# A new order of the work at two change-overs, and slot tables counted in tiles, in an attention / expert / mixing block

## The reference

```python
x = x + attn_a(layernorm(x), W_q, W_k, W_v, W_o)      # causal linear attention, H = 64
x = x + ffn(layernorm(x), router_W, router_b, W1, b1, W2, b2)
x = x + attn_b(layernorm(x), time_decay, mixes, Wk, Wv, Wr, Wo)   # scan over time, then a gate
x = x + ffn(layernorm(x), router_W, router_b, W1, b1, W2, b2)     # the same weights again

def attn_a(x):              # phi(u) = elu(u) + 1
    q, k, v = phi(x @ W_q), phi(x @ W_k), x @ W_v
    S_t = S_{t-1} + k_t v_t^T;  z_t = z_{t-1} + k_t
    return ((S_t q_t) / max(z_t . q_t, 1e-6)) @ W_o

def ffn(x):                 # 8 experts, each token to one of them
    probs = softmax(x @ router_W + router_b);  top1 = argmax(probs)
    h = relu(x @ W1[top1] + b1[top1])                  # 128 -> 512
    return probs[top1] * (h @ W2[top1] + b2[top1])     # 512 -> 128

def attn_b(x):
    state_t = x_t + state_{t-1} * d;  prev_t = state_{t-1}
    v_in, r_in = mixes of x_t and prev_t
    return sigmoid(r_in @ Wr^T) * ((v_in @ Wv^T) @ Wo^T)
```

## Time and profile before

| | before |
|---|---|
| median of 3 runs | 356.7 us |
| profiled execution, its time | 358.61 us |
| profiled execution, span from first to last instruction | 356.9 us |
| mean granted TensorE clock | 0.94 of full |
| PE busy | 301.4 us (84%) |
| DVE busy | 256.4 us (72%) |
| POOL busy | 202.2 us (57%) |
| ACT busy | 137.4 us (39%) |

### The profile page before, as it was taken

How to read it: one execution, slowest core, us unless ns; L and a number is a source line. 1 busy time by engine, 2 the same in 40 slices (tenths; PEclk the granted TensorE clock), 3 DMA queues, 4 the chain that set the end, 5 groups by cost and what they waited for, 6 DMA issues and landing times.

```text
span 356.9 us, 9023 instructions
## 1 busy us (share of the span) xinstructions
PE 301.4 (84%) x2137; PEld 255.4 (72%) x2137; DVE 256.4 (72%) x1046; ACT 137.4 (39%) x407; POOL 202.2 (57%) x247
## 2 busy tenths in 40 slices
PE   1898999975778899999996979678696999999970
PEld 1366676654668799999934768567395989999960
DVE  4748799999587877787626778686458787777750
ACT  3645565421223344444304653422122334454420
POOL 4834378885545774455425456887423676545550
PEclk9999999995898999999998999989859899999995
DMA  7992001105636788777144000111644778877500
GB/s 201 251 200 27 1 18 39 40 30 180 154 110 174 211 219 237 196 207 167 38 121 116 0 3 23 38 38 48 195 121 123 211 206 229 227 195 200 155 8 0
DMA packets 42610, 44.22 MB, mean 124 GB/s; under 512 B 7120, under 2 KB 29905, under 8 KB 42560
## 3 DMA queue, kind: packets, MB, share of 16 engines
q10 hardware_dynamic: 11808, 20.71, 22.6%
q1 hardware_dynamic: 26176, 14.39, 17.4%
q0 software_dynamic: 4576, 8.54, 6.7%
HBM read 33.06 MB, written 11.53 MB: 125 GB/s over the span
## 4 chain that ended last, share of the span: by engine, by line
PE 53%; DVE 18%; POOL 11%; issue 8%; DMA 3%; ACT 3%; DVEq 1%; SPq 0%; POOLq 0%; ACTq 0%
PE pair L1324 17%; PE pair L1310 14%; POOL sorted L449 5%; PE bank L1310 4%; DVE stats L706 3%; PE pair L1154 2%; POOL rstd L408 2%; PE pair L1178 2%; PE pair L1215 2%; PE pair L1136 2%; DVE hT L1022 2%; POOL rows L423 1%; PE pair L1144 1%; PE pair L1200 1%; PE pair L1301 1%
## 5 line engine op out<-in xcount | busy, mean ns | idle before, releaser
L1324 PE MATMUL pair<-w2s,hT 128*128 x624 | 86.3, 283 | 1.7 <-ACT hT L655 0.6
L449 POOL DMA_INDIRECT sorted<-rows,place x64 | 65.3, 1020 | 29.0 <-issue 14.7
L1324 PEld LDWEIGHTS pair<-w2s,hT 128*128 128x128 f32 x624 | 78.4, 197 | 4.0 <-issue 3.8
L1310 PE MATMUL pair<-xsT,w1s 128*128 128x128 f32 x472 | 69.4, 286 | 1.0 <-ACT xsT L649 0.8
L1310 PEld LDWEIGHTS pair<-xsT,w1s 128*128 128x128 f32 x472 | 62.6, 202 | 1.7 <-ACT xsT L649 1.7
L462 POOL DMA_INDIRECT out<-ys,xs x39 | 38.1, 976 | 32.3 <-DVE ys L1033 25.8
L462 POOL DMA_INDIRECT x_mid<-ys,xs x39 | 38.1, 978 | 31.7 <-DVE ys L1033 27.4
L1022 DVE TENSOR_SCALAR hT<-pair,w1s 128x128 f32<-128x128 f32 x156 | 47.0, 343 | 3.4 <-PE pair L1310 3.2
L1014 DVE SCALAR_TENSOR_TENSOR xs<-b2b,xs 128x128 f32<-128x128 f32 x78 | 27.6, 353 | 21.7 <-DVE xsn L1006 19.5
L1033 DVE SCALAR_TENSOR_TENSOR ys<-pair,xs 128x128 f32<-128x128 f32 x78 | 27.2, 349 | 13.7 <-PE pair L1324 13.5
L706 DVE BATCH_NORM_STATS2 stats<-rows 128x6 f32<-128x128 f32 x128 | 27.5, 277 | 10.4 <-DMA rows<-x_mid 6.7
(11 more groups left out here) (159 smaller groups left out, 513.6 us busy)
## 6 DMA issues: line engine op xcount, KB each, us to landing
w1s<-in_L_ffn_W_b ACTq DMA_DIRECT2D x78, 258.0 KB
xs<-sorted SPq DMA_DIRECT2D x78, 66.0 KB, 3.4
rows<-in_L_attn_a_x SPq DMA_DIRECT2D x8, 256.0 KB, 4.0
w2s<-in_L_ffn_W SPq DMA_DIRECT2D x8, 256.0 KB, 5.7
rows<-x_mid SPq DMA_DIRECT2D x8, 256.0 KB, 4.8
sorted<-pad SPq DMA_DIRECT2D x30, 66.0 KB, 3.5
sorted<-rows,place POOLq DMA_INDIRECT x64, 2.4
x_mid<-ys,xs POOLq DMA_INDIRECT x39, 3.5
```

The lines of the kernel that those rows point to most:

```text
L449: pool.indirect_dma_start(sorted_rows[l], bass.IndirectOffsetOnAxis(ap=place[:, t:t + 1], axis=0), rows[:, t, :], None).then_inc(s_sent[l] ...
L1310: mm = nc.tensor.matmul(bank[2 + 2 * half + i % 2][:, c * P:(c + 1) * P], w1s[i % NW][:, f:f + P], xsT[i % NB][:], start=True, stop=True)
L1324: mm = nc.tensor.matmul(bank[6 + i % 2][:, 0:P], hT[i % NB][:, c], w2s[:, bass.ds(e, 1), c, :].rearrange("p o d -> p (o d)"), start=(c == ...
```

## The change

It alters eight things; nothing of what is computed changes.

1. **Tables in tiles.** `slot_table` counts in tiles of 128 rows. Part 0 has 3 instructions (5 before), part 1 has 3 (3 in stage 0, 5 later), part 2 has 3. What a stage passes to the next (`cover`, `taken`, `gone`, `behind`) is a part 3 of its own with 3 instructions in stage 0 and 4 in stage 1. SP's load takes a tile number. At the start POOL makes one more small constant (`capt8`) and DVE two (`whole8`).
2. **First change-over, DVE.** Slot 8 becomes `last_attn_slot`: `denominators(6)`, `mask_scores(7)`, the first table (until then at the end of slot 7), `add_state(7)`, `placed(4)`, `add_attention(6)`, `choose(5)`.
3. **First change-over, into the experts.** `placed(5)` comes after the first three `norm_rows`, and `moments(6)` comes with `moments(7)` after `hidden(0)`.
4. **First change-over, PE.** `project_out(7)` is the last but one step of attention slot 8, ahead of `count(5)`. Before `first(0)` PE waits for `placed(5)` to have read the counts.
5. **ACT, both.** Only 2 of the first 4 weight loads come before the last copy (`evac_o(7)`, `evac_x2T(7)`), the other 2 after it.
6. **Second change-over, DVE.** The first table comes ahead of `choose(5)`, `moments(6)` goes into the experts, `keep_logits` comes ahead of `hidden(0)`.
7. **Second change-over, PE.** `logits(6)` comes ahead of `count(5)`; `keep_clock(6)` becomes `keep_clock(2)`; `transpose_x2(7)` comes ahead of the two `turn`s and `logits(7)` ahead of `first(0)`.
8. **Expert slots.** Table parts move: stage 0's part 3 and stage 1's part 0 to slot 0, stage 1's parts 1 and 2 to slot 1, stage 1's part 3 to slot 4.

```diff
@@ slot_table @@
+                    so_far = posb[b][0:1, GT * len(ROUTE_BATCHES[b])]
+                    step(nc.vector.scalar_tensor_tensor(out=ntile[:, s, 0], in0=so_far, scalar=1.0 / P,
+                                                        in1=whole8[:, int(final)], op0=ALU.mult, op1=ALU.add))
...
+                if 3 in parts:
+                    step(nc.vector.tensor_scalar(cover[:, s, 1:E + 1], cumt[:, s], float(count), None, ALU.min))
...
@@ DVE @@
+            def last_attn_slot():
+                denominators(LASTG - 1)
+                mask_scores(LASTG)
+                slot_table(0, 0, (0, 1, 2))
+                add_state(LASTG)
+                placed(0, AS, LASTB - 2)
+                add_attention(LASTG - 1)
+                choose(0, AS, LASTB - 1)
...
@@ DVE mix_slot @@
+                if k == NG - 1:
+                    slot_table(1, 0, (0, 1, 2))
                 if (b := batch_ending(ROUTE_BATCHES, k - 2)) is not None and b < LASTB:
                     choose(1, BS, b)
-                if 0 <= k - 1 < LASTG:
+                if 0 <= k - 1 < LASTG - 1:
                     dve.wait_ge(BS["xnew"], k)
                     moments(BS, 2, k - 1)
...
-                if k == NG - 1:
-                    slot_table(1, 0)
@@ DVE experts @@
                 if l == 0:
+                    placed(0, AS, LASTB - 1)
                     denominators(LASTG)
                     add_attention(LASTG)
+                else:
+                    keep_logits()
                 hidden(0)
-                if l == 1:
-                    keep_logits()
-                slot_table(l, 1, (0,))
                 dve.wait_ge(S["xnew"], NG)
-                moments(S, 2, LASTG)
+                for g in ROUTE_BATCHES[LASTB]:
+                    moments(S, 2, g)
...
-                    if i < 2:
-                        slot_table(l, 1, (i + 1,))
+                    if i == 0:
+                        slot_table(l, 0, (3,))
+                        slot_table(l, 1, (0,))
+                    if i == 1:
+                        slot_table(l, 1, (1, 2))
+                    if i == TABLE_AT - 1:
+                        slot_table(l, 1, (3,))
@@ PE @@
                 if k == NG:
+                    project_out(LASTG)
                     count(AS, LASTB - 1, bank[2])
...
+                if l == 1:
+                    transpose_x2(LASTG)
                 turn(0)
                 turn(1)
                 if l == 1:
-                    transpose_x2(LASTG)
+                    logits(LASTG)
+
+                pe.wait_ge(S["posb"], 2 * (LASTB - 1) + 1)
                 first(0)
                 if l == 0:
-                    project_out(LASTG)
...
-            keep_clock(6)
+            keep_clock(2)
```

116 lines of the change are left out of this document (63 added, 53 removed).

## The result

The changed kernel took 348.94 us (median of 4 runs, 348.26 to 349.19), the kernel before 357.36 us in the same comparison (356.46 to 358.87): a ratio of 0.9757, 95% interval 0.9717 to 0.9798, or 8.4 us less. The forecast was 348.2 us, with 8.5 us from the sum. The profiled execution took 349.11 us with a span of 347.4, against 358.61 and 356.9 before.

A forecast was written before the change was run, and what follows sets the result against it. PE was taken to pace the long middle of the experts, with gains only at the two change-overs, where the chain runs through DVE. 2.9 + 5.7 - 0.1 = 8.5 us off the 356.7 median gave 348.2, range 345.4 to 352.2.

The forecast's parts named there:

- the likeliest case: Whole kernel: both change-overs gain as summed, 348.2 us, own range 346.3 to 350.6; chance 0.60.
- up to here nothing is won: First change-over, up to the third `xsn`: it ends at 88.95 us, as before (89.0).
- first change-over 2.9: First change-over: 2.95 us gained behind the third `xsn`, expert-slot tables costing about 0.05; bounds nothing and 3.8 us.
- The wait of `prod` and `rtab`: First change-over: `prod` waits for POOL's product until 81.44 us, so `rtab` comes at 82.1, 0.65 us later than before.
- The end of the 3.78 us wait: First change-over, behind the third `xsn`: DVE's 3.78 us idle for PE's `first(0)` and last output product can be won.
- That SP would stand there until group 3's rows had landed: Second change-over: table ends at 245.35 us, but SP waits for group 3's rows, landing by 246.0.
- the clock holds: Rival: the second `first(0)` runs at full clock, 1.4 us more gained, 346.9 us; chance 0.13.
- Rows were to land 3.1 us after issue: First change-over: rows issued at 83.1, 84.3 and 85.5 us land at 86.2, 87.4 and 88.6.
- One half only: Rival: late loads at either change-over, rows or a weight by 2 us, lose about 3 us: 351.3 us; chance 0.17.
- the prediction's own signs of being wrong: Waits for xs or w1s over 1 us in expert slots 0 to 3, last `zT` moved, or clock 0.50 after slot 9.
- No change: Rival: batch 6's chain ends at a fixed time, so slot 17 gives the lead back: 356.7 us; chance 0.06.
- slower by the clock: Rival: fewer filling matmuls leave PE at half clock deep into the experts, slots 3.8 us: 361 us; chance 0.04.

The follow-up runs named there:

- e12: The changed kernel unaltered, run again beside its halves on one chip: 348.26 us, ratio 0.9781 to the kernel before.
- e14: The changed kernel with the second change-over put back, including six filling matmuls, tables still in tiles: 353.00 us, ratio 0.9896 to the kernel before.
- e13: The changed kernel with the first change-over put back, tables in tiles and second change-over kept: 347.74 us, ratio 0.9736 to the kernel before.
- e3: The kernel before with only its tables counted in tiles, all in the old places: ratio 0.9881 to the kernel before.
- e1: The changed kernel with the first change-over put back, tables in tiles and second change-over kept, on another chip: ratio 0.9841 to the kernel before.
- e5: The changed kernel with POOL's second row product of group 7 ahead of group 3's last send: ratio 0.9772 to the kernel before.
- e9: The changed kernel with one weight load instead of two first at the first change-over, two behind the `xsT` copies: ratio 0.9722 to the kernel before.

## Why the prediction was right in its time and wrong in its parts

**The time.** 8.5 us were forecast; 8.4 and 8.2 us were measured, within the range and by the likeliest case. The closeness is partly luck: in the first pair of traces the first change-over gave 0.8 us less than forecast, the second 0.5 more, and the stretches outside both 1.2. By stretches the change-overs are worth, where 2.9 and 5.7 were forecast, 2.7 us (49.33 less 46.6, the mean of after, e12 and e14) and 7.1 (57.70 less 50.6, the mean of after, e12 and e13). That they sum to 9.8 and not 8.4 fits the profiled execution of before, which at 358.61 was itself 1.3 us above its median: part of what the trace of before loses at the second change-over is its half-clock `first(0)`.

**The step whose account failed** is the one that closes "up to here nothing is won". I set the new order against the old one as the trace of before shows it, in which the last table instruction lost 1.0 us to POOL's product. I had seen that loss and priced it, but took it as a feature of the old order. It was there by 0.07 us, and the shorter table of point 1 ends it without any new order (3.12 us in e3, e1 and e13 alike). The gain that I booked as "first change-over 2.9" is therefore 1.9 us for the tables and 0.2 to 1.4 for the order, in the times -1.3 with 2.1 either way. At the second one I forecast 5.7 and the stretches give 7.1: 2.0 of them are there without the order, though more than half of that is the clock, and of the other 5.1 some 3.6 go with the four filling matmuls. The sum lets `turn(1)` begin at 252 and so rests on their being gone, but gives them no term; they appear only as a risk to the clock. The change should have been summed in four parts and not two: the tables, each order, and the filling.

**Steps that held.** The wait of `prod` and `rtab` at +0.65 (measured +0.57, and gone in e5). The end of the 3.78 us wait. At the second change-over `rtab` is 5.3 us earlier and the third `xsn` 4.8, forecast 4.8 and 4.2. That SP would stand there until group 3's rows had landed, 0.65 us behind the table, held only nearly: the last send (at 239.20) lands in 2.3 us, at 241.49, and `rtab` ends at 241.55, so the two come together, and SP's first load follows the table by the same 0.75 us as before (242.30; before 250.87 behind 250.12). `hidden(0)` 4.4 us earlier forecast, measured 5.5, of which 0.85 is the full clock of `first(0)`: the rival "the clock holds", given 0.13, happened there in part. Slots at 1.91 us, and no change of them. The start: 0.17 us later, forecast 0.1.

**A term mis-sized.** Rows were to land 3.1 us after issue; at the first change-over the three `xsn` began 3.7, 4.2 and 4.2 us after their loads were issued (at 81.05, 82.22 and 83.37), each after a wait for them. The third ended 0.9 us later than before, not at the same place, and the fourth stands 2.1 us ahead in place of 2.95. e9 shows that 0.8 of it goes with one of the two weights issued in between. The landings that the trace of before holds are those of later loads (at 90.72 and 91.87, 2.9 and 3.3 us), when one weight was beside them and not a row of them; the median of a window with another mixture is not the price.

**The rivals.** "One half only" named late loads as its mechanism; none of the waits of 2 us that it asked for is there. (Of the prediction's own signs of being wrong, one did occur in small: the `xsn` of slot 1 waited 1.39 us for its rows, over the 1 us allowed, which is the mis-sized term above. And the last z scan did move, by 2.0 us, which is PE's speed ahead of the second.) But one half only, the second, is what the times of e13 and e12 can't rule out, for another reason. "No change" and "slower by the clock" are excluded: from 283.94 on the lead stays at 9.5 us. The low clock did not go away, though. The work that stood in the window from 260 to 266 us, at 0.50 before, now lies some 9.5 us earlier, and there (250.5 to 256.5) the clock was 0.72; it was 0.50 again from 265 to 271 us and 1.00 from 274 on.

**What stays open.** Whether the first half is worth anything at all: 0.2 to 1.4 us by stretches, nothing by the times of one chip and 2 to 3 us, within the noise, by those of another. What the four filling matmuls cost in the times. Why `first(0)` of l = 1 gets full clock in one execution and half in another. Why two chips take 24 and 28 us longer with the same instructions; only their extra waits of PE were seen.
